# Splitting the scale-and-clamp of a row maximum: one VectorE operation added after the first half, one removed after the second

## The chip, the cores and the metric

The kernel runs on one core of one Trainium2 chip. The metric is device time in microseconds (us), the median of three runs. A core has five engines that run side by side, each with a queue that it works through in order: TensorE (PE, matrix products), VectorE (DVE), ScalarE (ACT), GpSimd (POOL) and SyncE (SP, which here issues every DMA). They wait for one another on semaphores.

## What is computed

A cross-attention block and a quantised feed-forward block, each behind a layer norm and with a residual, on x of 8 x 1024 x 512. Only the second block bears on the change:

```python
def _act_quant(x):
    scale = 127.0 / jnp.clip(jnp.max(jnp.abs(x), axis=-1, keepdims=True), 1e-05)
    xq = jnp.clip(jnp.round(x * scale), -128.0, 127.0) / scale
    return x + jax.lax.stop_gradient(xq - x)

def _bitlinear(x, w):
    return jnp.einsum('bsi,oi->bso', _act_quant(x), _weight_quant(w))
gate = jax.nn.silu(_bitlinear(x, w_gate))
up = _bitlinear(x, w_up)
return _bitlinear(gate * up, w_down)
```

`gate * up` is called h below. It is 2048 wide, and each of its rows is quantised by its own largest absolute value before the product with `w_down`.

## The kernel before

The 8192 rows are 64 tiles of 128 rows; a row lies in one SBUF partition. Weights stay on chip. A tile goes through two halves of the program, attention first and, six tiles behind, the feed-forward part, so that one turn of the loop works on several tiles at once. Of one tile the feed-forward part does this:

- `stats` and `rstd` (DVE, then POOL) find mean and inverse deviation; `x_scale` (DVE, L1085 to L1092) centres the row, finds its maximum and writes three scales, one of them `sgu[:, 1]`, by which `up` has to be multiplied; `quant_x` (ACT) and `copy_x` (DVE) quantise, and a DMA transposes.
- `gate_up` (PE, L1327) makes gate and up in four slices of 512 columns; `silu` (ACT, L818) and `mult` (DVE, L1032) turn each slice into a slice of h in SBUF, still without the scale of up.
- `h_part` (DVE, L1036) takes the absolute maximum of columns 0 to 1023 of h into `hm[:, 0:1]`, `h_max` (L1040) that of columns 1024 to 2047 into `hm[:, 1:2]`. L1041 joins both into `am`, L1042 multiplies by `sgu[:, 1]` and clamps from below at EPS into `t2`, L1044 inverts it and L1045 makes `c2`, the factor of the quantisation. All of these but the first work on one number in each partition.
- `quant_h` (ACT, L827) scales h by `c2`, `copy_h` (DVE, L1050) casts it, a DMA transposes it, `down` (PE, L1346) multiplies, and `final` (DVE, L1024) adds the result to the row. `d_scale` (POOL, L660) makes its scale from `t2`.

Of the attention half these pieces are met below: `e_sum` (DVE, L1073 to L1077), `p_norm` (POOL, L679), `p_hi` (ACT, L845), `p_lo` (POOL, L687), `add_bo` (POOL, L673), `add_x` (DVE, L1104), `x_norm` (DVE, L1056) and `s_max` (DVE, L1063 and L1067).

There is extra work in three blocks of eight tiles (the attention's weights are folded for two batches at once): `pair_X` on PE (L1254, L1259, which wait for `final`), `j_wide` (L781, L787) and `j_hi` (L794) on ACT, `j_lo` (L698) on POOL. The first block lies in the opening. Tiles with this work are called fold tiles here, the others plain tiles.

The order of each queue comes from `put(time, piece)`: pieces are sorted by a planned time. For the opening (up to about 340 us) the order is instead written out by hand, in a list for each engine. A piece is one function, and what it issues stays together. `link(...)` around a DVE operation counts a semaphore up at its end and makes the next DVE operation wait for it; without it, the next operation may begin before the last one has ended.

Of the kernel before, what the change touches and what calls it, by code (L numbers as in the profile page):

```python
# [13 lines left out]
EPS = 1e-5  # L14
L = 6
R = 11
W = 8

ALU = mybir.AluOpType
ACT = mybir.ActivationFunctionType  # L20
AX_X = mybir.AxisListType.X
# [7 lines left out]
def xattn_ffn(nc, x, ctx_768, Wq, Wk, Wv, Wo, bo, w_gate, w_up, w_down, out):  # L29
# [11 lines left out]
    with ExitStack() as ctx:  # L41
        def sb(name, shape, dt):
            return ctx.enter_context(nc.sbuf_tensor(name, shape, dt))
# [15 lines left out]
        h = FF[:, 0:4096].rearrange("p (s n) -> p s n", s=2)  # L59
# [61 lines left out]
        am = sb("am", [P, 2, W], F32)  # L121
        hm = sb("hm", [P, 4], F32)
# [3 lines left out]
        sgu = sb("sgu", [P, 2, W], F32)  # L126
        t2 = sb("t2", [P, W], F32)
# [768 lines left out]
        def _(eng):  # L896
# [3 lines left out]
            def link(ins):  # L900
                ch[0] += 1
                ins.then_inc(v_ch, 1)
                eng.wait_ge(v_ch, ch[0])
# [129 lines left out]

            def h_part(i):
                eng.wait_ge(v_h, 4 * i + 2)
                eng.tensor_reduce(hm[:, 0:1], h[:, i % 2, 0:1024], AX_X, ALU.max, apply_absolute_value=True)  # L1036

            def h_max(i):
                eng.wait_ge(v_h, 4 * i + 4)
                link(eng.tensor_reduce(hm[:, 1:2], h[:, i % 2, 1024:2048], AX_X, ALU.max, apply_absolute_value=True))  # L1040
                link(eng.tensor_tensor(am[:, 1, i % W:i % W + 1], hm[:, 0:1], hm[:, 1:2], ALU.max))  # L1041
                link(eng.tensor_scalar(t2[:, i % W:i % W + 1], am[:, 1, i % W:i % W + 1], sgu[:, 1, i % W:i % W + 1], EPS,  # L1042
                                       ALU.mult, ALU.max))
                link(eng.reciprocal(r2[:, i % W:i % W + 1], t2[:, i % W:i % W + 1]))  # L1044
                eng.tensor_scalar(c2[:, i % W:i % W + 1], r2[:, i % W:i % W + 1], sgu[:, 1, i % W:i % W + 1], 127.0, ALU.mult,  # L1045
                                  ALU.mult).then_inc(v_c2, 1)
# [88 lines left out]
            for s in range(FIRST, LAST + 1):  # L1135
                i, j = s, s + L
                if 0 <= i - 2 < NT:
                    put(at(s, .02) if s < NT - 1 else at(max(s, NT), (.122, .125, .127)[s - NT + 1]), final, i - 2)
                if 0 <= j + 1 < NT:
                    put(norm_at(s, .05, "stats"), stats, j + 1, 0)  # L1140
                if 0 <= i + 1 < NT:
                    put(x_at(i + 1, 0), stats, i + 1, 1)
                if 0 <= i - 1 < NT:
                    late = .41 if i == NT - 1 else 0
                    put(at(s, late + .11), copy_h, i - 1, 0)
                    put(at(s, late + .12), copy_h, i - 1, 1)
                if 0 <= j + 1 < NT:
                    put(norm_at(s, .3, "norm"), x_norm, j + 1)
                if 0 <= j < NT:
                    put(at(s, .4), s_max, j)  # L1150
                    put(at(s, .6), e_sum, j)
                if 0 <= i + 1 < NT:
                    put(x_at(i + 1, 2), x_scale, i + 1)
                    put(x_at(i + 1, 4), copy_x, i + 1)
                if 0 <= j - 1 < NT:
                    put(at(s, .8), add_x, j - 1)
                if 0 <= i < NT:
                    for f, w in enumerate((.15, .45, .65, .94)):
                        put(at(s, w), mult, i, f)
                    put(at(s, .62), h_part, i)  # L1160
                    put(at(s, .95), h_max, i)
# [233 lines left out]
```

## Time and profile before

| what | value |
|---|---|
| median of three runs | 1132.76 us (1132.17 to 1136.36) |
| profiled execution, its time | 1135.72 us |
| profiled execution, span of the core | 1133.9 us |
| PE, DVE, ACT, POOL busy | 94%, 88%, 66%, 44% |
| granted PE clock, mean of the profiled execution | 0.984 |
| maximum of h's first half (L1036) | 64 times, 1209 ns |
| maximum of h's second half (L1040) | 64 times, 1218 ns |
| joining both maxima (L1041) | 64 times, 527 ns |
| scale and clamp (L1042) | 64 times, 214 ns |

A row of a timeline has start, duration, engine, line, operation, what is written and read, and in brackets the idle time before it with what ended it. Consecutive DVE operations overlap a little where no wait stands between them, so the distance from one start to the next, and not the duration, is what an operation takes of its engine. A chain row names what the end of the run was waiting for at that moment.

### The profile page before, as it was taken

Reading aid. Unit: us, or ns where it says so; the run is one execution under the profiler, and the core shown is the slowest. Engines: PE = TensorE matmul, PEld = TensorE weight load, DVE = VectorE, ACT = ScalarE, POOL = GpSimd, SP = SyncE. Lnnn points to the kernel's source line nnn. Section 1 sums busy time; section 2 is a strip of 40 time slices with the busy share of each in tenths; the row PEclk is TensorE's granted clock in tenths of the full one; section 3 lists DMA queues with packets and bytes.
Section 4 is the critical chain, followed back from the end, with each engine's and each line's share of the span. In section 5 each row is a group of like instructions: output and inputs, shape, how many; then the busy total and the mean of one; then the engine's idle time right before and its main releaser. Section 6 shows DMA issues by size and latency. Waiting matters only on the chain.

```text
span 1133.9 us, 17119 instructions
## 1 busy us (share of the span) xinstructions
PE 1071.5 (94%) x5308; PEld 482.7 (43%) x5370; DVE 1003.0 (88%) x2097; ACT 744.4 (66%) x955; POOL 497.5 (44%) x641
## 2 busy tenths in 40 slices
PE   6668999999999999999999999999999999999998
PEld 3323344444344444444444444444444444444443
DVE  5888989978989998988999989889999999998886
ACT  2888657767756676676666666766766666665543
POOL 1046544556544445455443454454444444444110
PEclk9769999999999999999999999999999999999999
DMA  9798653564355454354455544544555544554334
GB/s 349 218 257 163 110 116 75 89 136 103 73 118 122 103 117 112 79 112 107 99 106 118 117 106 94 104 108 85 115 117 120 101 106 103 121 108 93 72 73 98
DMA packets 355962, 133.79 MB, mean 118 GB/s; under 512 B 332448, under 2 KB 332960, under 8 KB 355360
## 3 DMA queue, kind: packets, MB, share of 16 engines
q1 hardware_dynamic: 355872, 132.70, 53.1%
q8 instruction: 43, 0.70, 0.3%
q14 instruction: 47, 0.39, 0.1%
HBM read 34.08 MB, written 16.78 MB: 45 GB/s over the span
## 4 chain that ended last, share of the span: by engine, by line
PE 38%; DVE 19%; issue 6%; POOL 4%; ACT 4%; DMA 1%; SPq 0%; ACTq 0%; DVEq 0%; POOLq 0%
PE ps L1327 17%; PE ps L1346 8%; PE ps L1266 4%; PE ps L1267 4%; PE ps L1269 4%; DVE hm L1040 3%; DVE FF L1032 2%; DVE FF L1085 2%; POOL rs L653 2%; DVE bns L1018 1%; POOL MV L698 1%; DVE hm L1036 1%; ACT FF L818 1%; DVE xr L1024 1%; DVE am L1041 1%
## 5 line engine op out<-in xcount | busy, mean ns | idle before, releaser
L1327 PE MATMUL ps<-wgT,FF 128*128 128x512 bf16 x1024 | 262.9, 379 | 1.6 <-ACT FF L818 1.0
L1327 PE MATMUL ps<-wW,FF 128*128 128x512 bf16 x1024 | 262.9, 379 | 1.6 <-DVE FF L1032 1.6
L1346 PE MATMUL ps<-wW,FF 128*128 128x512 bf16 x962 | 218.7, 379 | 9.5 <-DMA FF<-FF 4.8
L827 ACT ACTIVATE FF<-FF,c 128x1024 int16<-128x1024 f32 x128 | 141.1, 1141 | 124.1 <-DVE c L1045 121.5
L818 ACT ACTIVATE FF<-ps,sgu 128x512 f32<-128x512 f32 x256 | 173.4, 680 | 63.5 <-PE ps L1327 62.0
L1032 DVE TENSOR_TENSOR FF<-FF,ps 128x512 f32<-128x512 f32 x256 | 173.4, 681 | 38.0 <-ACT FF L818 18.9
L679 POOL TENSOR_TENSOR AT<-AT,rd 128x512 f32<-128x512 f32 x64 | 67.4, 1053 | 298.3 <-DVE rd L1077 295.1
L1346 PEld LDWEIGHTS ps<-wW,FF 128*128 128x128 bf16 x1024 | 99.7, 98 | 128.4 <-issue 7.2
L1327 PEld LDWEIGHTS ps<-wW,FF 128*128 128x128 bf16 x1024 | 99.7, 98 | 123.9 <-DVE FF L1032 4.9
L1327 PEld LDWEIGHTS ps<-wgT,FF 128*128 128x128 bf16 x1024 | 98.8, 98 | 124.9 <-issue 3.2
L667 POOL TENSOR_TENSOR xhl<-xn,xhl 128x512 f16<-128x512 f32 x64 | 74.1, 1158 | 75.4 <-ACT xhl L834 75.4
L687 POOL TENSOR_TENSOR AT<-AT 128x512 f16<-128x512 f32 x64 | 74.6, 1166 | 50.3 <-POOL AT L679 37.3
L651 POOL TENSOR_SCALAR ve<-mv 128x1 f32<-128x1 f32 x128 | 45.2, 353 | 116.9 <-DVE mv L1019 116.9
L1018 DVE BATCH_NORM_STATS2 bns<-xr 128x6 f32<-128x512 f32 x128 | 86.3, 675 | 3.2 <-DMA xr<-in_x 3.1
L845 ACT ACTIVATE AT<-AT 128x512 f16<-128x512 f32 x64 | 40.1, 627 | 73.7 <-POOL AT L679 73.5
L653 POOL TENSOR_TENSOR rs<-ve,half 128x1 f32<-128x1 f32 x128 | 83.5, 652 | 10.7
L1266 PE MATMUL ps<-MV,xT 128*128 128x512 f16 x192 | 75.8, 395 | 10.3 <-DMA xT<-xhl 9.1
L673 POOL TENSOR_TENSOR xr<-xr,bo_sb 128x512 f32<-128x512 f32 x64 | 81.7, 1277 | 0.0
L1040 DVE TENSOR_REDUCE hm<-FF 128x1 f32<-128x1024 f32 x64 | 77.9, 1218 | 1.9
L1266 PE MATMUL ps<-MV,pT 128*128 128x512 f16 x192 | 73.6, 383 | 4.3 <-issue 2.9
L1036 DVE TENSOR_REDUCE hm<-FF 128x1 f32<-128x1024 f32 x64 | 77.4, 1209 | 0.1
L1267 PE MATMUL ps<-MV,xT 128*128 128x512 f16 x192 | 75.8, 395 | 0.0
(142 smaller groups left out, 1730.7 us busy)
## 6 DMA issues: line engine op xcount, KB each, us to landing
xr<-in_x SPq DMA_DIRECT2D x64, 256.0 KB, 2.8
out<-xr SPq DMA_DIRECT2D x64, 256.0 KB, 2.3
FF<-in_L_ffn_w_gate SPq DMA_DIRECT2D x4, 1024.0 KB, 13.4
wW<-in_L_ffn_w_up SPq DMA_DIRECT2D x4, 1024.0 KB, 14.2
FF<-in_L_ffn_w_down SPq DMA_DIRECT2D x4, 1024.0 KB, 6.1
FF<-FF SPq DMA_TRANSPOSE x192, 3.2
MV<-in_L_xattn_Wq SPq DMA_DIRECT2D x1, 1024.0 KB, 5.7
MV<-in_L_xattn_Wo SPq DMA_DIRECT2D x1, 1024.0 KB, 12.3
```

The costliest lines, as they stand in the source:

```text
L653: eng.tensor_tensor(rs[:, t % W:t % W + 1], ve[:, t % W:t % W + 1], half[:, :], ALU.pow).then_inc(end, 1)
L673: eng.tensor_tensor(xr[:, t % R, :], xr[:, t % R, :], bo_sb[:, :], ALU.add).then_inc(g_xb, 1)
L818: eng.activation(h[:, i % 2, f * 512:(f + 1) * 512], G[n % 2][:, :], ACT.Silu, scale=sgu[:, 0, i % W:i % W + 1]).then_inc(a_si, 1)
L827: eng.activation(q16h[:, 1024 * z:1024 * z + 1024], h[:, t % 2, 1024 * z:1024 * z + 1024], ACT.Copy, scale=c2[:, t % W:t % W + 1]).then_in ...
L1018: link(eng.bn_stats(bns[:, k, t % 2, :], xr[:, t % R, :]))
L1032: eng.tensor_tensor(hh, hh, U[n % 2][:, :], ALU.mult).then_inc(v_h, 1)
L1036: eng.tensor_reduce(hm[:, 0:1], h[:, i % 2, 0:1024], AX_X, ALU.max, apply_absolute_value=True)
L1040: link(eng.tensor_reduce(hm[:, 1:2], h[:, i % 2, 1024:2048], AX_X, ALU.max, apply_absolute_value=True))
L1266: eng.matmul(bank[:, :], T[:, k, :], hi[k], start=(k == 0), stop=False)
L1267: eng.matmul(bank[:, :], T[:, k, :], lo[k], start=False, stop=False)
L1327: mm = eng.matmul(bank[n % 2][:, :].rearrange("p (o f) -> p o f", o=4), qxT[:, i % 2, k, :], w[:, 4 * f:4 * f + 4, k, :], start=(k == 0), ...
L1346: mm = eng.matmul(y_bank(i)[:, :], hT[:, i % 2, c, :], wdT[:, c, :], start=(c == 0), stop=(c == 15))
```

## The change

`h_part` now waits for its own maximum, by a link, and then multiplies it by `sgu[:, 1]` and clamps it at EPS, into `hm[:, 2:3]`. In `h_max` the operation that joined the two maxima is gone; the following one multiplies the second maximum by `sgu[:, 1]` and takes the larger of that and `hm[:, 2:3]`. It has two scalars read from SBUF, where it had one and a constant. `am` is no longer written there. PE, ACT, POOL and SP have the same instructions in the same order.

```diff
             def h_part(i):
                 eng.wait_ge(v_h, 4 * i + 2)
-                eng.tensor_reduce(hm[:, 0:1], h[:, i % 2, 0:1024], AX_X, ALU.max, apply_absolute_value=True)
+                link(eng.tensor_reduce(hm[:, 0:1], h[:, i % 2, 0:1024], AX_X, ALU.max, apply_absolute_value=True))
+                eng.tensor_scalar(hm[:, 2:3], hm[:, 0:1], sgu[:, 1, i % W:i % W + 1], EPS, ALU.mult, ALU.max)
 
             def h_max(i):
                 eng.wait_ge(v_h, 4 * i + 4)
                 link(eng.tensor_reduce(hm[:, 1:2], h[:, i % 2, 1024:2048], AX_X, ALU.max, apply_absolute_value=True))
-                link(eng.tensor_tensor(am[:, 1, i % W:i % W + 1], hm[:, 0:1], hm[:, 1:2], ALU.max))
-                link(eng.tensor_scalar(t2[:, i % W:i % W + 1], am[:, 1, i % W:i % W + 1], sgu[:, 1, i % W:i % W + 1], EPS,
+                link(eng.tensor_scalar(t2[:, i % W:i % W + 1], hm[:, 1:2], sgu[:, 1, i % W:i % W + 1], hm[:, 2:3],
                                        ALU.mult, ALU.max))
```

The DVE queue around `h_part` of a fold tile, before:

```order
L1092 TENSOR_SCALAR c<-r,rs 128x1
L1036 TENSOR_REDUCE hm<-FF 128x1
L1032 TENSOR_TENSOR FF<-FF,ps 128x512
L1099 CAST FF<-FF 128x512
L1073 TENSOR_REDUCE den<-AT 128x8
```

And after:

```order
L1092 TENSOR_SCALAR c<-r,rs 128x1
L1036 TENSOR_REDUCE hm<-FF 128x1
L1037 TENSOR_SCALAR hm<-hm,sgu 128x1
L1032 TENSOR_TENSOR FF<-FF,ps 128x512
L1099 CAST FF<-FF 128x512
L1073 TENSOR_REDUCE den<-AT 128x8
```

The scale and clamp of the first half now stands between its maximum and the third `mult`. The DVE queue around `h_max` of the same tile, before:

```order
L1104 SCALAR_TENSOR_TENSOR xr<-ps,bck,xr 128x512
L1032 TENSOR_TENSOR FF<-FF,ps 128x512
L1040 TENSOR_REDUCE hm<-FF 128x1
L1041 TENSOR_TENSOR am<-hm 128x1
L1042 TENSOR_SCALAR t<-am,sgu 128x1
L1044 RECIPROCAL r<-t 128x1
L1045 TENSOR_SCALAR c<-r,sgu 128x1
L1024 SCALAR_TENSOR_TENSOR xr<-ps,sd,xr 128x512
```

And after (the second maximum is now on line 1041 of the file):

```order
L1104 SCALAR_TENSOR_TENSOR xr<-ps,bck,xr 128x512
L1032 TENSOR_TENSOR FF<-FF,ps 128x512
L1041 TENSOR_REDUCE hm<-FF 128x1
L1042 TENSOR_SCALAR t<-hm,sgu 128x1
L1044 RECIPROCAL r<-t 128x1
L1045 TENSOR_SCALAR c<-r,sgu 128x1
L1024 SCALAR_TENSOR_TENSOR xr<-ps,sd,xr 128x512
```

One operation fewer stands between the second maximum and `c2`; the rest of the queue is as it was.

## Rows read from the trace of the kernel before

**Rows 1.** The page: busy time of each engine, share of the span, instructions.

```profile
PE 1071.5 (94%) x5308; PEld 482.7 (43%) x5370; DVE 1003.0 (88%) x2097; ACT 744.4 (66%) x955; POOL 497.5 (44%) x641
```

**Rows 2.** Stretches of one tile: length, busy PE, PEld, DVE, ACT, POOL; clock, DMA.

```profile
624.05:639.59 15.54, 15.49 (x73) 7.05 (x72) 14.46 (x31) 9.98 (x12) 6.75 (x10) 1.00 0.59 111
...
705.30:722.61 17.31, 16.44 (x97) 7.66 (x96) 15.25 (x31) 12.36 (x18) 9.02 (x12) 1.00 0.54 100
...
773.99:791.02 17.03, 16.43 (x85) 7.27 (x85) 15.25 (x31) 12.15 (x16) 9.01 (x12) 1.00 0.50 102
```

**Rows 3.** Chain that ended last, in a fold tile: start us, length us, what.

```profile
717.14 1.04 DVE hm L1036
...
722.61 0.65 DVE am L1041
...
731.51 1.41 DVE FF L1085
```

**Rows 4.** Timeline of DVE in the same fold tile.

```profile
717.06 1.21 DVE L1036 TENSOR_REDUCE hm<-FF 128x1 f32<-128x1024 f32 x1
718.18 0.68 DVE L1032 TENSOR_TENSOR FF<-FF,ps 128x512 f32<-128x512 f32 x1
...
722.61 0.64 DVE L1041 TENSOR_TENSOR am<-hm 128x1 f32<-128x1 f32 x1
723.29 0.21 DVE L1042 TENSOR_SCALAR t<-am,sgu 128x1 f32<-128x1 f32 x1
723.53 0.16 DVE L1044 RECIPROCAL r<-t 128x1 f32<-128x1 f32 x1
723.73 0.21 DVE L1045 TENSOR_SCALAR c<-r,sgu 128x1 f32<-128x1 f32 x1
723.86 0.74 DVE L1024 SCALAR_TENSOR_TENSOR xr<-ps,sd,xr 128x512 f32<-128x512 f32 x1
```

**Rows 5.** Timeline of POOL in the same fold tile.

```profile
722.08 1.15 POOL L687 TENSOR_TENSOR AT<-AT 128x512 f16<-128x512 f32 x1 [0.80 <-POOL AT L679]
723.20 1.26 POOL L673 TENSOR_TENSOR xr<-xr,bo_sb 128x512 f32<-128x512 f32 x1
...
725.50 0.21 POOL L651 TENSOR_SCALAR ve<-mv 128x1 f32<-128x1 f32 x1 [0.76 <-DVE mv L1019]
...
731.47 1.16 POOL L698 TENSOR_TENSOR MV<-FF,MV 128x512 f16<-128x512 f32 x1 [0.99 <-ACT MV L794]
```

**Rows 6.** A DVE group with constants only: busy us, mean ns; idle before it.

```profile
L1003 DVE TENSOR_SCALAR wst<-wst 128x1 f32<-128x1 f32 x3 | 0.5, 153 | 0.1
```

**Rows 7.** PE's waits from 400 to 1080 us: total us, times, longest.

```profile
PE ps L1259 <- DVE xr L1024: 5.0, 8, 0.8
```

**Rows 8.** Timeline of DVE in the opening, small operations beside a POOL operation.

```profile
286.71 0.21 DVE L1088 TENSOR_SCALAR t<-am,rs 128x1 f32<-128x1 f32 x1
...
287.15 0.68 DVE L1091 TENSOR_SCALAR sgu<-wst,t 128x2 f32<-128x2 f32 x1
```

**Rows 9.** Timeline of POOL at the same time.

```profile
286.65 1.16 POOL L687 TENSOR_TENSOR AT<-AT 128x512 f16<-128x512 f32 x1
```

**Rows 10.** L1041 and L1085: shortest, median and longest of 64 in ns.

```profile
L1041 DVE TENSOR_TENSOR am<-hm x64: 158/641/1087, 124.6 to 1121.0; 128x1 f32<-128x1 f32 x64
...
L1085 DVE TENSOR_SCALAR FF<-xr,mv x64: 448/481/1530, 94.5 to 1104.3; 128x512 f32<-128x512 f32 x64
```

**Rows 11.** Timeline of DVE in the opening: a long L1041.

```profile
155.50 1.09 DVE L1041 TENSOR_TENSOR am<-hm 128x1 f32<-128x1 f32 x1
```

**Rows 12.** Chain between opening and first full block of fold tiles.

```profile
361.49 1.20 DVE hm L1036
...
365.23 0.17 DVE am L1041
```

**Rows 13.** Chain over the last tiles.

```profile
1068.15 0.17 DVE am L1041
...
1118.52 0.52 issue
```

## What I predict

> **What bounds the kernel now.** I read the engines' shares first. PE is busy for 94% of the span and DVE for 88% [rows 1], which leaves open who waits for whom, so the next view is one tile at a time. There are two sorts of tile. A plain tile takes 15.54 us, and PE is busy in 15.49 of them [rows 2]: there PE sets the pace, and the chain that ended last, followed through such a stretch, consists of PE lines alone. A saving on DVE is worth nothing there. A fold tile takes 17.31 us (17.03 in the later ones of a block, where `pair_X` has its second form), and PE is busy for 16.44 of it [rows 2]. PE stands still in it, 0.8 us at a time, in front of `pair_X`, waiting for `final` on DVE [rows 7]. In a fold tile the chain goes round in a loop: down DVE from `x_scale` (L1085) over `h_part` (L1036), `e_sum`, `add_x`, `mult` and `h_max` to L1041 and L1042, then over `final`, `stats` and `rstd`, a `j_lo`, the next `j_wide` and `silu`, and back to L1085 [rows 3]. So in the fold tiles, and not in the others, what DVE does between the two maxima and `c2` is time.
>
> The second thing to see is what L1041 costs. It takes the larger of two numbers in each partition, and it lasts from 158 to 1087 ns, median 641 [rows 10]. In the fold tile it begins at 722.61 and ends at 723.25 [rows 4]. POOL's `p_lo` began at 722.08 and lasted 1.15 us, to 723.23 [rows 5]. In the fold tiles, L1041 ends 0.02 us after `p_lo`: it is held by it, and the hold is three quarters of its time. The Trainium skill (SBUF — State Buffer, section Who interferes with whom) gives a mechanism: a DVE instruction with two SBUF inputs contends with a GpSimd instruction that reads SBUF, and the later one blocks until the first is done. L1041 reads two SBUF tensors, so the trace agrees, with 0.64 us held against 0.16 free.
>
> **The change part by part.**
>
> *The joined maximum goes.* From the start of L1041 to that of L1042 it takes 723.29 - 722.61 = 0.68 us in a fold tile [rows 4]; where nothing holds it, 0.16 + 0.04 = 0.20 us.
>
> *L1042 reads a second scalar from SBUF.* No tiny operation with two of them is in the trace. The bounds: nothing, if both are fetched together; and what the first one costs, 214 ns of L1042 [rows 4] less 153 ns of L1003 with constants only = 61 ns [rows 6]. I take 0.06 us, the same step again. So L1041's removal is worth 0.68 - 0.06 = 0.62 us where it was held and 0.14 us where it wasn't.
>
> *Is the new form held in its turn?* Without L1041 the scale and clamp stands inside `p_lo`'s time. In the opening L1088, of the same shape (128x1, one scalar from SBUF), began at 286.71 inside a `p_lo` that ran from 286.65 to 287.81, and took its usual 0.21 us; L1091 (128x2) began at 287.15 in the same `p_lo` and took 0.68 us, to its end [rows 8, 9]. And L1042, L1044 and L1045 now lie inside `add_bo`, which begins at 723.20, with nothing lost [rows 4, 5]. So one-element operations with one tensor are not held.
>
> *`h_part` grows by an operation and a wait.* Now the next operation starts 718.18 - 717.06 = 1.12 us after it, before it has ended [rows 4]. With the link it must end: 1.21 us, then the 0.03 us that lie between L1042's end and L1044's start, then the new operation, which takes 723.86 - 723.73 = 0.13 us from its start to the next one's, as L1045 does [rows 4]. Together 1.37 us, 0.25 more. Behind it on DVE stand the third `mult`, `copy_x`, `e_sum`, `add_x`, the last `mult` and `h_max`; for these wait ACT, PE and, on `e_sum`, POOL's `p_norm` and `p_lo`.
>
> *A fold tile:* -0.62 + 0.25 = -0.37 us. There are two blocks of eight on the chain, 410 to 531 us and 670 to 792 us; L1041 lies on it 16 times, L1036 14 times (rows 3 show one of each): 16 x 0.62 - 14 x 0.25 = 9.9 - 3.5 = 6.4 us. What becomes late next? PE waits 0.8 us for `final`, so it has 0.8 to give. POOL is idle for 0.76 us before `rstd` (L651) [rows 5]; its `p_lo` and `add_bo` come 0.25 later and DVE's `stats` 0.37 earlier against the start of the loop, so 0.76 - 0.62 = 0.14 us is left. Thin, but enough.
>
> *Between the opening and the first block (340 to 410 us)* the chain has four more L1041, two free ones as at 365.23 and two held, and one L1036 whose full 1.20 us count already [rows 12]: 2 x 0.14 + 2 x 0.61 - (1.37 - 1.20) = 1.3 us.
>
> *The last tiles* have four free L1041 on the chain, 4 x 0.14 = 0.6 us; the last `h_part` has 0.52 us of idle behind it, which covers its 0.25 [rows 13].
>
> *Plain tiles:* nothing. PE is the pace, and DVE, at 14.46 of 15.54 us [rows 2], gains 0.37 of slack. Were that cover gone, the price would be 0.
>
> *The opening (120 to 340 us, 13 tiles)* has its order written out by hand, and the chain can't be followed through it. Four L1041 are held there (0.59 to 1.09 us, [rows 11] is the longest), nine are free. If every L1041 counted and no `h_part`, it would give about 3.7 - 0.24 + 9 x 0.14 = 4.7 us; if every `h_part` counted and no L1041, it would cost 13 x 0.25 = 3.3 us. A hold removed here may also pass to the next cast or `x_norm`. I take 0, near the middle, and keep both ends.
>
> **The sum:** 6.4 + 1.3 + 0.6 + 0 = 8.3 us. From the profiled execution's 1135.72 us that gives 1127.4. That execution lies 3.0 us above the median of the runs, 1132.76, and the median is what I forecast: 1132.76 - 8.3 = 1124.5 us.
>
> **The rivals.**
>
> *The opening pays.* The fold tiles give their 6.4 us, the tiles around them 1.9, and the opening takes all of its 3.3: 1132.8 - 5.0 = 1127.7 us, which is within 0.5%. For it: DVE is as busy there as elsewhere. Against it: four holds of up to 1.09 us go in the same stretch.
>
> *The hold passes to the scale and clamp.* L1042 would start 0.68 earlier and 0.25 later, at 722.86 in the clock of rows 4, and end with `p_lo`, itself 0.25 later, at 723.48; now it ends at 723.50. The fold tiles would gain nothing, and I would get 1132 us. Rows 8 and 9 speak against it, since L1088 is the same form. The Trainium skill (VectorE: DVE Perf Modes, section What auto-detection actually checks) bears on this: a one-source operation in SBUF takes both ports if the outermost non-unit dimensions are even or equal. Read so that one element counts as equal, it would make L1042 contend; the 128x2 row agrees with the rule and the 128x1 row with the reading that one element doesn't qualify.
>
> *POOL becomes the loop (slower).* The place is POOL between `p_norm` and `rstd` in the fold tiles. Its operations hang on `e_sum`, which comes 0.25 us later. The slack there is 0.14 us by my count, and POOL's durations are rough; if it is used up, by more than 0.14 us of extra POOL time, the gain after L1041 ends in POOL's queue. At full size the loop then runs from `h_part` over `p_norm` to `rstd` and carries the 0.25 with no gain: 16 x 0.25 = 4.0 us, and with the opening's 3.3 it is 1132.8 + 7.3 = 1140.1 us. Against it: POOL is busy for only 9.02 of 17.31 us [rows 2].
>
> *A second hold falls too (much faster).* `x_scale`'s L1085 begins at 731.51 [rows 3] and lasts 1.41 us because POOL's L698 began at 731.47 [rows 5], 0.04 us ahead. Its median over the run is 0.48 [rows 10]. If DVE came first, a fold tile would save another 0.9 us: 14 x 0.9 = 13 us, 1111.9. Against it: both hang on the same `silu`, so both move together.
>
> **How the numbers follow.** Forecast 0.61, the opening pays 0.19, the hold passes on 0.05, POOL becomes the loop 0.09, the second hold falls 0.06. The opening's own bounds put the forecast between 1132.8 - 13.0 = 1119.8 and 1127.8. A range from 1119 to 1133 holds the forecast and the first two rivals, 0.85, and leaves out the slower case and the much faster one. A measurement can tell about 0.5%, or 5.7 us, from no change. The faster side is the forecast, less a little of its upper end, and the last rival, 0.64; the same side is the first two rivals and that upper end, 0.27; slower 0.09.
>
> **What would show it.** Right: no `am<-hm` operation; fold tiles of about 16.94 and 16.66 us and plain tiles still at 15.54; the distance from the second maximum's start to `c2` about 0.6 us shorter; t2's operation at 0.21 to 0.28 us; L1036 to the next operation 1.37; PE's wait before `pair_X` near 0.45 and POOL's idle before L651 near 0.14. Wrong: t2's operation at 0.6 us (the hold has passed on); POOL with no idle time before L651, and fold tiles at 17.3 or more; or an opening that has become over 3 us longer. If plain tiles change at all, my reading that PE alone bounds them is wrong.

## The result

| | median | lowest to highest | runs |
|---|---|---|---|
| before | 1132.76 us | 1131.46 to 1136.36 | 5 |
| changed kernel | 1123.41 us | 1121.14 to 1126.73 | 5 |

The ratio is 0.9913, with a 95% interval of 0.9884 to 0.9941: the kernel became faster by 0.6 to 1.2%. Forecast were 1124.5 us. A second comparison on another occasion gave 1122.22 against 1131.25 us, ratio 0.993 (0.9906 to 0.9954).

The shares of the changed kernel, which answer to [rows 1] (busy time, share of the span, instructions). DVE has the same number of instructions as before and 16 us less to do:

```profile
PE 1066.2 (95%) x5308; PEld 481.0 (43%) x5370; DVE 987.3 (88%) x2097; ACT 745.1 (66%) x955; POOL 498.5 (44%) x641
```

Stretches of one tile in it, as in [rows 2]: two fold tiles, of the first and second form, and a plain tile.

```profile
695.20:712.16 16.96, 16.91 (x99) 7.87 (x98) 14.89 (x31) 12.37 (x18) 9.04 (x12) 1.00 0.55 102
745.80:762.47 16.67, 16.43 (x85) 7.29 (x84) 14.89 (x32) 12.15 (x16) 9.03 (x12) 1.00 0.47 103
614.60:630.14 15.54, 15.49 (x73) 7.02 (x73) 14.06 (x32) 9.98 (x12) 6.76 (x10) 1.00 0.55 111
```

The fold tiles went from 17.31 to 16.95 us and from 17.03 to 16.67; the plain tile kept its 15.54 although DVE does 0.4 us less in it. The DVE timeline of a fold tile, to be laid beside [rows 4]:

```profile
706.36 1.21 DVE L1036 TENSOR_REDUCE hm<-FF 128x1 f32<-128x1024 f32 x1
707.60 0.21 DVE L1037 TENSOR_SCALAR hm<-hm,sgu 128x1 f32<-128x1 f32 x1
707.73 0.68 DVE L1032 TENSOR_TENSOR FF<-FF,ps 128x512 f32<-128x512 f32 x1
...
710.19 0.68 DVE L1032 TENSOR_TENSOR FF<-FF,ps 128x512 f32<-128x512 f32 x1
710.90 1.22 DVE L1041 TENSOR_REDUCE hm<-FF 128x1 f32<-128x1024 f32 x1
712.16 0.27 DVE L1042 TENSOR_SCALAR t<-hm,sgu 128x1 f32<-128x1 f32 x1
712.47 0.16 DVE L1044 RECIPROCAL r<-t 128x1 f32<-128x1 f32 x1
```

From L1036 to the third `mult` it is now 707.73 - 706.36 = 1.37 us, as forecast. From the start of the scale and clamp to L1044 it is 712.47 - 712.16 = 0.31 us, where L1041 and L1042 together had taken 723.53 - 722.61 = 0.92 in [rows 4]. That operation begins inside `p_lo`, which runs from 711.63 to 712.79, and isn't held:

```profile
711.63 1.16 POOL L687 TENSOR_TENSOR AT<-AT 128x512 f16<-128x512 f32 x1 [0.80 <-POOL AT L679]
712.75 1.28 POOL L673 TENSOR_TENSOR xr<-xr,bo_sb 128x512 f32<-128x512 f32 x1
714.00 0.31 POOL L660 TENSOR_SCALAR sd<-t,wst 128x1 f32<-128x1 f32 x1
714.44 0.21 POOL L651 TENSOR_SCALAR ve<-mv 128x1 f32<-128x1 f32 x1
...
715.92 0.57 POOL L653 TENSOR_TENSOR rs<-ve,half 128x1 f32<-128x1 f32 x1
717.14 1.15 POOL L698 TENSOR_TENSOR MV<-FF,MV 128x512 f16<-128x512 f32 x1 [0.65 <-ACT MV L794]
```

Of the 64 executions of this scale and clamp 49 begin while an operation of POOL is running. All 64 (shortest, median, longest in ns) are alike:

```profile
L1042 DVE TENSOR_SCALAR t<-hm,sgu x64: 272/273/275, 118.9 to 1107.8; 128x1 f32<-128x1 f32 x64
```

PE waits for `final` in front of `pair_X` for 0.4 to 0.5 us at most, where it was 0.8 in [rows 7]; 0.45 was forecast.

To see where the time went I followed one event, the start of `c2`'s operation, through all 64 tiles of each trace and compared the distances with those of before (the column "before" has its time in us, the others the difference to it; minus is less time):

| stretch | before | changed | changed, second profile | share in the forecast |
|---|---|---|---|---|
| start to tile 0 | 125.2 | -5.8 | -6.4 | none |
| tiles 0 to 13 (opening) | 224.9 | -0.8 | -1.3 | 0 |
| 13 to 17 | 61.2 | -0.8 | -0.8 | -1.3 |
| 17 to 29 (block of fold tiles) | 198.3 | -2.9 | -2.9 | -3.2 |
| 29 to 33 (plain) | 62.2 | 0.0 | 0.0 | 0 |
| 33 to 45 (block of fold tiles) | 198.3 | -2.9 | -2.9 | -3.2 |
| 45 to 57 (plain) | 186.5 | +0.1 | +0.1 | 0 |
| 57 to 63 (end) | 65.1 | -0.4 | -0.5 | -0.6 |
| 0 to 63 together | 996.5 | -7.6 | -8.3 | -8.3 |

The first row isn't the change's, but for some tenths: the only changed operations in it are tile 0's own `h_part` and `h_max`, and from the start of its second maximum to `c2` it is 1.75 us instead of 1.88. Tile 0's `x_scale`, ahead of which nothing of the change runs, already began at 89.4 and 88.5 us instead of 94.5. What that is, is looked at in the experiments.

### The profile page after: what moved, and what is told of

It is laid out like the page before. It is cut to its first block, busy times and chain, and to the rows that moved or that the text cites. A ratio compares the mean times of both kernels' runs of the same rounds, so it can differ in the third digit from the quotient of the medians.

```text
span 1120.6 us, 17119 instructions
## 1 busy us (share of the span) xinstructions
PE 1066.2 (95%) x5308; PEld 481.0 (43%) x5370; DVE 987.3 (88%) x2097; ACT 745.1 (66%) x955; POOL 498.5 (44%) x641
## 4 chain that ended last, share of the span: by engine, by line
PE 49%; DVE 15%; POOL 3%; issue 3%; ACT 2%; DMA 1%; ACTq 0%; SPq 0%; DVEq 0%; POOLq 0%
PE ps L1327 22%; PE ps L1346 11%; PE ps L1266 5%; PE ps L1269 5%; PE ps L1267 5%; DVE FF L1032 2%; DVE hm L1041 2%; DVE FF L1085 2%; DVE hm L1036 2%; POOL rs L653 1%; POOL MV L698 1%; DVE xr L1024 1%; DVE am L1086 1%; DVE xr L1104 1%; DVE bns L1018 1%
## 5 line engine op out<-in xcount | busy, mean ns | idle before, releaser
L679 POOL TENSOR_TENSOR AT<-AT,rd 128x512 f32<-128x512 f32 x64 | 67.4, 1053 | 306.8 <-DVE rd L1077 303.7
L667 POOL TENSOR_TENSOR xhl<-xn,xhl 128x512 f16<-128x512 f32 x64 | 74.1, 1158 | 74.2 <-ACT xhl L834 74.2
L687 POOL TENSOR_TENSOR AT<-AT 128x512 f16<-128x512 f32 x64 | 74.6, 1166 | 49.5 <-POOL AT L679 37.3
L651 POOL TENSOR_SCALAR ve<-mv 128x1 f32<-128x1 f32 x128 | 45.5, 356 | 99.1 <-DVE mv L1019 96.8
L653 POOL TENSOR_TENSOR rs<-ve,half 128x1 f32<-128x1 f32 x128 | 83.7, 654 | 10.7
L1266 PE MATMUL ps<-MV,xT 128*128 128x512 f16 x192 | 75.8, 395 | 7.5 <-DMA xT<-xhl 6.4
L673 POOL TENSOR_TENSOR xr<-xr,bo_sb 128x512 f32<-128x512 f32 x64 | 81.9, 1281 | 0.0
L1041 DVE TENSOR_REDUCE hm<-FF 128x1 f32<-128x1024 f32 x64 | 78.0, 1218 | 1.9
L1036 DVE TENSOR_REDUCE hm<-FF 128x1 f32<-128x1024 f32 x64 | 77.4, 1209 | 0.1
L834 ACT ACTIVATE xhl<-xn 128x512 f16<-128x512 f32 x64 | 40.0, 626 | 54.5 <-DVE xn L1056 49.6
## 6 DMA issues: line engine op xcount, KB each, us to landing
FF<-in_L_ffn_w_gate SPq DMA_DIRECT2D x4, 1024.0 KB, 13.3
```

The source lines that it names most:

```text
L653: eng.tensor_tensor(rs[:, t % W:t % W + 1], ve[:, t % W:t % W + 1], half[:, :], ALU.pow).then_inc(end, 1)
L673: eng.tensor_tensor(xr[:, t % R, :], xr[:, t % R, :], bo_sb[:, :], ALU.add).then_inc(g_xb, 1)
L687: eng.tensor_tensor(phl[:, 1, :], E[:, j % 2, :], phl[:, 0, :], ALU.subtract).then_inc(g_pl, 1)
L1036: link(eng.tensor_reduce(hm[:, 0:1], h[:, i % 2, 0:1024], AX_X, ALU.max, apply_absolute_value=True))
L1266: eng.matmul(bank[:, :], T[:, k, :], hi[k], start=(k == 0), stop=False)
```

## The experiments

The theory to test has three parts: L1041 was slow because GpSimd held it; `h_part`'s new wait costs 0.25 us on the path of a fold tile; POOL is close to becoming the bound there. Rivals are that it is one operation and one wait fewer that counted, that the new wait is hidden, and that the hold had another cause.

### Only the join, without a second SBUF tensor

```diff
-link(eng.tensor_tensor(am[:, 1, i % W:i % W + 1], hm[:, 0:1], hm[:, 1:2], ALU.max))
+link(eng.tensor_scalar(am[:, 1, i % W:i % W + 1], hm[:, 1:2], hm[:, 0:1], None, ALU.max))
```

> The kernel before with one edit: L1041 joins the two maxima as an operation with one SBUF tensor and one scalar read from SBUF, in place of one with two SBUF tensors. Number of operations, waits and h_part are as before. My theory (L1041 is slow because a GpSimd operation that reads SBUF holds it): L1041 falls from a median of 641 ns to about 214 ns and is never held; start of L1041 to start of L1042 goes from 0.68 to 0.25 us, fold tiles from 17.31 to 16.88 and from 17.03 to 16.60 us, plain tiles stay at 15.54; in all about 16 x 0.43 = 6.9 us plus under 1 us around the blocks: 1125 us, ratio 0.993. Rival (what counted was one operation and one semaphore wait fewer ahead of c2): L1041 stays near 0.64 us, fold tiles 17.31 and the ratio 1.000.

Measured: 1123.7 us against 1130.61, ratio 0.9934 (0.9915 to 0.9953). Fold tiles 16.90 and 16.62 us. L1041 in all its runs, against [rows 10]:

```profile
L1041 DVE TENSOR_SCALAR am<-hm x64: 213/214/215, 119.4 to 1107.3; 128x1 f32<-128x1 f32 x64
```

With the number of operations and waits unchanged, the same join is 0.43 us shorter (median 214 ns for 641) and the fold tiles by 0.41. That settles it against the rival: what counted was the kind of operand, not the number of operations. The whole effect of the change can be had from this one line: from tile 0 to tile 63 it gives 8.5 us, where the change gives 7.6 and 8.3.

### Only the first half of the change

```diff
 def h_part(i):
-    eng.tensor_reduce(hm[:, 0:1], h[:, i % 2, 0:1024], AX_X, ALU.max, apply_absolute_value=True)
+    link(eng.tensor_reduce(hm[:, 0:1], h[:, i % 2, 0:1024], AX_X, ALU.max, apply_absolute_value=True))
+    eng.tensor_scalar(hm[:, 2:3], hm[:, 0:1], sgu[:, 1, i % W:i % W + 1], EPS, ALU.mult, ALU.max)
```

> The kernel before with the first half of the change alone: h_part waits for its maximum and makes the scaled and clamped value, which nobody reads; h_max is as before, with the held L1041. My sum: L1036 to the operation behind it but one 1.37 us instead of 1.12, fold tiles 17.56 and 17.28 us, 14 x 0.25 = 3.5 us more in the blocks, and between 0 and 3.3 us more in the opening: 1136 to 1139 us, ratio 1.003 to 1.006. Rival (the wait is hidden, because DVE idles later in the tile waiting for silu): fold tiles stay at 17.31, ratio 1.000.

Measured: 1137.04 us against 1130.61, ratio 1.0049 (1.0031 to 1.0067). Fold tiles 17.57 and 17.29 us, each 0.26 longer; the two blocks +1.9 us each. PE waits longer for `final` (total us, times, longest), against the 5.0 and 0.8 of [rows 7]:

```profile
PE ps L1260 <- DVE xr L1024: 7.0, 8, 1.1
```

So the price of the added wait and operation is as worked out, and it is paid on the path. But between tiles 0 and 13 the distance changed by 0.04 us in all, and between 13 and 17 by 0.05. Single tiles of the opening moved by up to 0.6 us either way, and two profiles of one kernel differ there by 0.5 to 0.8 us; so the wait costs well under the 3.3 us of the bound, and whether it costs exactly nothing can't be told.

### POOL has less to do, and DVE waits longer

```diff
-eng.tensor_tensor(phl[:, 1, :], E[:, j % 2, :], phl[:, 0, :], ALU.subtract).then_inc(g_pl, 1)
+n = 512 if j == 0 else 128
+eng.tensor_tensor(phl[:, 1, 0:n], E[:, j % 2, 0:n], phl[:, 0, 0:n], ALU.subtract).then_inc(g_pl, 1)
```

> The kernel before, with p_lo on POOL (L687) working on 128 of its 512 columns from the second tile on; the rest of the low half keeps what the first tile left there, so a part of the attention's low-order product is left out. DVE's instructions are the same. In a fold tile p_lo is followed at once by add_bo, which takes 1.26 us and also reads SBUF. If L1041 is held by whichever GpSimd operation is reading when it starts: p_lo ends before L1041 starts, add_bo begins some 0.7 us earlier and holds it in its place, until about 723.7 in the clock of the tile shown: L1041 gets LONGER, to 1.0 to 1.1 us instead of 0.64, and the fold tiles go to about 17.7 us, though POOL has less to do. Rival (L1041 waits for p_lo alone, by some dependence on it): 0.16 us and fold tiles of 16.8. Rival (its length has nothing to do with POOL): 0.64 us and 17.31.

Measured: 1142.92 us against 1131.57, ratio 1.0098 (1.0074 to 1.0122); fold tiles 17.82 and 17.55 us. POOL in a fold tile:

```profile
707.74 0.43 POOL L688 TENSOR_TENSOR AT<-AT 128x128 f16<-128x128 f32 x1 [0.80 <-POOL AT L679]
708.12 1.27 POOL L673 TENSOR_TENSOR xr<-xr,bo_sb 128x512 f32<-128x512 f32 x1
```

and the join (here L1042) beside it on DVE, with its durations over all runs:

```profile
708.26 1.14 DVE L1042 TENSOR_TENSOR am<-hm 128x1 f32<-128x1 f32 x1
...
L1042 DVE TENSOR_TENSOR am<-hm x64: 159/1139/1146, 120.9 to 1126.7; 128x1 f32<-128x1 f32 x64
```

`p_lo` takes 0.43 us instead of 1.15 and ends before the join starts; `add_bo` has begun 0.14 us ahead of it, runs to 709.39, and the join ends at 709.40. The hold doesn't belong to `p_lo` but to the GpSimd operation that is running when the join starts. The trace of before has it too: 47 of its 64 L1041 end 0.01 to 0.02 us behind the end of a POOL operation, on five different lines (L667, L673, L679, L687, L698), and the 15 that begin outside any take 158 to 160 ns. All five read and write SBUF, so no run here separates reading from writing. Taking work from POOL made the kernel 1% slower. The hold on two SBUF inputs is the behaviour that the Trainium skill states (SBUF — State Buffer, Who interferes with whom) for a DVE instruction with two SBUF inputs against a GpSimd instruction that reads SBUF; the trace agrees, with the join's end 0.01 us behind that of `add_bo`.

### The scale and clamp without its wait

The changed kernel, with the new operation moved from `h_part` to the head of `h_max` (not shown: `part_done = [0]` ahead of it, and the rest of `h_max`, which is unchanged):

```diff
 def h_part(i):
-    link(eng.tensor_reduce(hm[:, 0:1], h[:, i % 2, 0:1024], AX_X, ALU.max, apply_absolute_value=True))
-    eng.tensor_scalar(hm[:, 2:3], hm[:, 0:1], sgu[:, 1, i % W:i % W + 1], EPS, ALU.mult, ALU.max)
+    eng.tensor_reduce(hm[:, 0:1], h[:, i % 2, 0:1024], AX_X, ALU.max, apply_absolute_value=True).then_inc(v_ch, 1)
+    ch[0] += 1
+    part_done[0] = ch[0]
 def h_max(i):
+    eng.wait_ge(v_ch, part_done[0])
+    eng.tensor_scalar(hm[:, 2:3], hm[:, 0:1], sgu[:, 1, i % W:i % W + 1], EPS, ALU.mult, ALU.max)
```

> The changed kernel, but the scale and clamp of the first half's maximum isn't made in h_part: it stands at the head of h_max, just ahead of the second maximum, where the first maximum is long there. h_part has no wait any more. If my 0.25 us for h_part is right and is paid on the path: the new operation fits in the 0.1 us in which DVE waits for the last mult anyway, so fold tiles go from 16.95 to about 16.70 to 16.75 and from 16.67 to 16.42 to 16.5, in all 3 to 4 us below the changed kernel: about 1120 us, ratio to before 0.989. PE then waits about 0.2 us for final in a fold tile, so it is near its floor. Rival (POOL, whose idle time before L651 is down to 0.13 us in the changed kernel, has become the bound): fold tiles stay at 16.9, ratio 0.991.

Measured: 1117.13 us against 1130.61, ratio 0.9872 (0.985 to 0.9894). Fold tiles 16.70 and 16.43 us. DVE around the place:

```profile
706.92 0.68 DVE L1033 TENSOR_TENSOR FF<-FF,ps 128x512 f32<-128x512 f32 x1
707.52 0.21 DVE L1043 TENSOR_SCALAR hm<-hm,sgu 128x1 f32<-128x1 f32 x1
707.64 1.21 DVE L1045 TENSOR_REDUCE hm<-FF 128x1 f32<-128x1024 f32 x1
```

From the last `mult` to the maximum it is 707.64 - 706.92 = 0.72 us; in the changed kernel it is 710.90 - 710.19 = 0.71 without the operation. The operation is free here: DVE would otherwise stand until the `mult` has ended. The fold tiles came as expected, so the rival, POOL as the bound at 16.9, falls. These are two stretches of one fold tile each:

```profile
692.40:709.10 16.70, 16.70 (x99) 7.76 (x98) 14.71 (x32) 12.37 (x18) 9.03 (x12) 1.00 0.56 104
742.50:758.93 16.43, 16.43 (x86) 7.23 (x84) 14.72 (x32) 12.15 (x16) 9.04 (x12) 1.00 0.48 105
```

PE is busy for the whole of them, the chain that ended last runs through PE lines alone, and of the 0.2 us that PE was still to wait for `final` the view of its waits shows nothing. But 16.70 us isn't PE's own time. The chain has `pair_X` of the same tile and of the next (start us, length us, what):

```profile
694.21 0.78 PE ps L1258 x24
...
710.63 0.78 PE ps L1258 x24
```

That is 16.42 us from one to the next. The 16.70 is the distance from one `c2` to the next, so DVE's loop takes 0.28 us more than PE's work does. `c2` enters the second block 2.26 us ahead of `pair_X`. That lead shrinks to 1.73 us over a first distance of 16.95, and to 1.45, 1.16 and 1.02 us over the next three of 16.70. It just lasts until the tiles of the second form, where both take 16.43. So PE's pace is the bound of the block, to within 0.2 us for the seven distances between its eight `pair_X`, though `c2`'s distance doesn't show it.

### The clamp behind the reciprocal

The kernel before; `h_part` untouched, `sgu` with a third column for the scale over 127. Not shown are the lines that make this column, and `d_scale`, which now reads a weight scale that isn't divided by 127 and takes `t2` without the clamp; that differs only for a row whose scaled maximum lies under EPS:

```diff
-link(eng.tensor_tensor(am[:, 1, i % W:i % W + 1], hm[:, 0:1], hm[:, 1:2], ALU.max))
-link(eng.tensor_scalar(t2[:, i % W:i % W + 1], am[:, 1, i % W:i % W + 1], sgu[:, 1, i % W:i % W + 1], EPS,
-                       ALU.mult, ALU.max))
+link(eng.tensor_scalar(t2[:, i % W:i % W + 1], hm[:, 1:2], hm[:, 0:1], sgu[:, 2, i % W:i % W + 1],
+                       ALU.max, ALU.mult))
 link(eng.reciprocal(r2[:, i % W:i % W + 1], t2[:, i % W:i % W + 1]))
-eng.tensor_scalar(c2[:, i % W:i % W + 1], r2[:, i % W:i % W + 1], sgu[:, 1, i % W:i % W + 1], 127.0, ALU.mult,
-                  ALU.mult).then_inc(v_c2, 1)
+eng.tensor_scalar(c2[:, i % W:i % W + 1], r2[:, i % W:i % W + 1], 127.0 / EPS, sgu[:, 1, i % W:i % W + 1],
+                  ALU.min, ALU.mult).then_inc(v_c2, 1)
```

> The kernel before with the clamp moved: h_part as before; h_max takes the larger of both maxima and multiplies by the scale over 127 in one operation with two scalars read from SBUF; the clamp is made behind the reciprocal, in the operation that makes c2. So L1041 goes and nothing is added in the loop. Expected by my sum: 0.62 us per fold tile, 16.69 and 16.41 us, 16 x 0.62 = 9.9 us less in the blocks and some in the opening; PE waits 0.2 us in a fold tile. About 1121 us, ratio 0.989, 3 to 4 us below the changed kernel. Rival (POOL or PE bounds the fold tile by now): 16.9 us, ratio 0.991.

Measured: 1120.16 us against 1130.61, ratio 0.9906 (0.9886 to 0.9926); fold tiles 16.71 and 16.43 us, as in the kernel before this one. The rival at 16.9 falls here too. One operation fewer than that one in each tile buys nothing more: there the extra operation was free on DVE, and PE is the pace of the block in both. In total it is 3.0 us behind it, with intervals that overlap. Of the 5.4 us between the two profiled executions 3.8 lie ahead of tile 0's `c2`, 0.5 in the second block, where PE waits once for 0.64 us for a DMA, and 1.1 in the last tiles.

### The changed kernel again

No edit.

> The changed kernel once more, beside the two kernels below, on one chip. Ratio to before 0.991 to 0.993 as in the first comparison. Its fold tiles, 16.95 and 16.67 us, come out alike to 0.02 us; the time of the first tile's c2, which nothing of the change precedes, lies anywhere from 119 to 125 us as in the other executions so far, if that part is the setup's own scatter, and at 119.4 again if the change moves it.

> The changed kernel with the first half's scale and clamp at the head of h_max, once more, for a comparison with the changed kernel on one chip. If the h_part wait costs 0.25 us per fold tile and the opening about 1 us: 4 to 6 us below the changed kernel, ratio to before 0.987. If the first comparison had luck in the setup: the same tile times, but a ratio near 0.989.

Measured, on one chip: changed kernel 1122.22 us, ratio 0.993 (0.9906 to 0.9954); scale and clamp moved 1119.31 us, ratio 0.9899 (0.9878 to 0.9919); before 1131.25 us. The fold tiles are the same to 0.01 us as in the first profiles. The move is worth 2.9 us here, less than the 4 to 6 expected. From tile 0 to 63 the traces have 3.3: 3.4 in the two blocks, and nothing (0.2 more time) in the opening, where I had looked for 1. The first two profiles had 4.6, with 3.3 in the blocks and 1.1 in the opening, so the opening's part isn't settled by these; the blocks' part is. The expectation also says that nothing of the change precedes tile 0's `c2`; as said above, tile 0's own `h_part` and `h_max` do.

On the start: tile 0's `x_scale` and `c2` began at these times in the ten profiles, beside PE's granted clock and number of matmuls from 60 to 90 us:

| kernel | `x_scale` | `c2` | clock | matmuls |
|---|---|---|---|---|
| moved, second profile | 86.8 | 117.3 | 0.83 | 152 |
| changed, second profile | 88.5 | 118.8 | 0.83 | 144 |
| changed | 89.4 | 119.4 | 0.78 | 140 |
| moved | 89.6 | 119.5 | 0.83 | 140 |
| only the join | 89.6 | 120.1 | 0.83 | 140 |
| less POOL work | 90.8 | 121.5 | 0.77 | 113 |
| clamp behind the reciprocal | 93.0 | 123.3 | 0.72 | 84 |
| changed, with more POOL work (below) | 93.7 | 124.2 | 0.73 | 86 |
| only the first half | 93.6 | 124.2 | 0.73 | 86 |
| before | 94.5 | 125.2 | 0.73 | 84 |

The windows of before and of the changed kernel (columns as in [rows 2]):

```profile
60.00:90.00 30.00, 17.07 (x84) 6.14 (x82) 24.62 (x53) 24.67 (x29) 14.83 (x18) 0.73 1.08 247
...
60.00:90.00 30.00, 19.03 (x140) 7.61 (x141) 24.80 (x56) 24.52 (x30) 18.22 (x22) 0.78 1.03 246
```

Three of the profiles have the changed kernel's instructions up to `c2`: 118.8, 119.4 and 124.2 us. So the setup scatters by some 5 us from one execution to the next. Of the 13.3 us between the two profiled spans, 1133.9 and 1120.6, 5.8 lie ahead of tile 0's `c2`, and 5.2 of them are there already at its `x_scale`: that is scatter, not gain. Why the setup is quick in one execution and slow in another wasn't tried.

### POOL at its supposed decision point

```diff
 eng.tensor_scalar(sd[:, i % W:i % W + 1], t2[:, i % W:i % W + 1], wst[:, 2, 3:4], None,
                   ALU.mult).then_inc(g_sd, 1)
+eng.tensor_scalar(am[:, 1, i % W:i % W + 1], t2[:, i % W:i % W + 1], wst[:, 2, 3:4], None, ALU.mult)
```

> The changed kernel with a second, unused d_scale-like operation on POOL right behind d_scale (L660): same shape, some 0.3 us of POOL time, ahead of rstd (L651). It tests the slower rival, POOL as the bound of a fold tile, at its decision point. In the changed kernel POOL is idle for 0.13 us there. If that is the slack, 0.17 us of the added 0.3 comes through to the loop: fold tiles 17.12 and 16.84 us, 14 x 0.17 = 2.4 us more in the blocks, ratio to before about 0.994. If POOL has more slack than the trace shows: 16.95 and the ratio of the changed kernel. If it had none: 17.25.

Measured: 1125.2 us, ratio 0.9934 (0.9911 to 0.9958), and fold tiles of 16.95 and 16.67 us: no effect in the blocks at all. POOL in such a tile:

```profile
717.34 0.31 POOL L660 TENSOR_SCALAR sd<-t,wst 128x1 f32<-128x1 f32 x1
717.62 0.29 POOL L662 TENSOR_SCALAR am<-t,wst 128x1 f32<-128x1 f32 x1
717.87 0.22 POOL L651 TENSOR_SCALAR ve<-mv 128x1 f32<-128x1 f32 x1
718.17 0.66 POOL L653 TENSOR_TENSOR rs<-ve,half 128x1 f32<-128x1 f32 x1
...
720.48 1.16 POOL L699 TENSOR_TENSOR MV<-FF,MV 128x512 f16<-128x512 f32 x1 [0.61 <-ACT MV L795]
```

From `d_scale` to `j_lo` it is 720.48 - 717.34 = 3.14 us, and 3.14 in the changed kernel without the operation as well (714.00 to 717.14). The idle time that stands before `j_lo`, 0.65 us in the changed kernel, is 0.61 now; `j_lo` waits for ACT's `j_hi`. The expectation fell. But the test was milder than meant. From `d_scale` to L651 it is 0.53 us instead of 0.44, so only 0.09 us of the delay was left there, and the second L653 ended 2.52 us behind `d_scale` instead of 2.49, since the operations between had become shorter (0.76 to 0.66 and 0.55 to 0.49 us). The run shows that so much doesn't reach the tile; how much would isn't measured.

## Why the prediction was right, point by point

**What bounds the kernel.** Right in the main. Plain tiles stayed at 15.54 us with DVE's path up to 0.6 us shorter and 0.25 us longer; only with 0.5 us more of hold did they become 15.58. For the fold tiles the part of the loop on DVE, from `x_scale` to `c2`, was right; the part behind `c2` wasn't, as said under POOL below.

**The hold.** Right, and now shown from two sides: another kind of operand removes it (214 ns), another GpSimd operation takes it over (1139 ns).

**The second scalar.** Taken at 0.06 us; L1042 went from 214 to 273 ns, 0.059.

**The new form isn't held.** Right in 64 of 64 executions, 49 of them begun beside a running POOL operation, so the rival by which the hold passes on is out. By the Trainium skill's rule (VectorE: DVE Perf Modes, What auto-detection actually checks) a one-source operation in SBUF takes both ports if the outermost non-unit dimensions are even or equal. The rows fit the reading that one element a partition doesn't qualify: none of those was held, while L1091, with two elements, takes 227 to 231 ns in 59 of 64 executions and up to 1198 ns in the other five, all of which begin beside a POOL operation. Which port an operation took is in no trace.

**`h_part`.** Taken at 0.25 us more; 1.37 us measured, and 0.26 per fold tile where it was added alone.

**A fold tile.** -0.37 forecast, -0.36 measured (16.95 and 16.67 for 16.94 and 16.66). The blocks gave 2.9 us each and not 3.2, because the first tile of a block gave 0.19 instead of the 0.62 that I counted for a tile with only L1041 on the chain; the way out of a block gave another 0.2. In the changed kernel the first three `pair_X` of the second block start at 663.82, 680.24 and 696.73 us, 16.42 and 16.49 apart: there PE's own pace holds, and only then does the loop with its 16.95.

**340 to 410 us.** Mis-sized: 0.8 us for 1.3. I had added up L1041s on the chain as if each could be shortened in full without another wait taking over. Tiles 15 and 16 did give 0.62 and 0.73 us, but tile 17 went from 15.06 to 15.54, PE's pace in a plain tile, and took 0.48 back.

**The opening.** I took 0 and kept -4.7 to +3.3. It was -0.8 and -1.3 in two profiles of the same kernel, and -2.1 in the one with more POOL work, which has the same DVE instructions. The upper bound was far too high: 13 waits of 0.25 us cost 0.04 us together when they were added alone, and one and the same DVE queue scatters there by 1.4 us. The rival in which the opening pays 3.3 us is refuted by both; its time, 1132.8 - 5.0, should read 1127.8.

**The last tiles.** 0.6 forecast, 0.4 and 0.5 measured.

**POOL as the next bound.** The step that failed, though the sum didn't hang on it. I read POOL's idle time ahead of L651 as its slack, 0.14 us after the change, and 0.13 is there. But 0.28 us more work went in without a trace of it in the tile time. The chain that I followed led through `rstd` to `j_lo`, with an "issue" piece of 0.62 us between them. The timelines of the kernel before show another path from the same `c2`, which ends at 723.94 [rows 4], to the same `j_lo`. On ACT, `quant_h`, `silu`, `j_wide` and `j_hi`:

```profile
723.98 2.19 ACT L827 ACTIVATE FF<-FF,c 128x1024 int16<-128x1024 f32 x2 [2.03 <-DVE c L1045]
726.08 0.67 ACT L818 ACTIVATE FF<-ps,sgu 128x512 f32<-128x512 f32 x1
726.64 0.82 ACT L787 ACTIVATE FF<-ps,fwd 128x256 f32<-128x256 f32 x2
727.50 0.63 ACT L794 ACTIVATE MV<-FF 128x512 f16<-128x512 f32 x1
```

and on POOL the end of `rstd`, and `j_lo`:

```profile
726.98 0.57 POOL L653 TENSOR_TENSOR rs<-ve,half 128x1 f32<-128x1 f32 x1
728.21 1.16 POOL L698 TENSOR_TENSOR MV<-FF,MV 128x512 f16<-128x512 f32 x1 [0.65 <-ACT MV L794]
```

ACT works without a gap from `c2` to 728.13, and `j_lo`, whose only wait in the program is for `j_hi`, starts 0.08 us later; `rstd` has been over for 0.66 us. So the loop goes over ACT here, and `final`, `stats` and `rstd` lie beside it, with that much to spare on POOL. A chain that crosses half a microsecond of nothing has taken the wrong branch. The sum was right all the same, since both branches start from `c2` and what the change touches stands ahead of it. Nothing was run that lengthens or shortens ACT's part alone.

**The second hold.** `x_scale` still takes 1.39 to 1.40 us in a fold tile and starts 0.04 to 0.05 us behind POOL's operation. The order didn't flip.

**The total.** Tile by tile the gain is 7.6 to 8.3 us for 8.3 forecast. The medians differ by 9.4 and 9.0; the rest is within their intervals, and the setup alone scatters by more.

## What to carry to other kernels

A tiny operation whose duration varies as this one's did, from 158 to 1087 ns, is likely held by something: lay its end beside the ends of the other engines' operations before changing the algorithm around it. Here the cure was to pass one of two one-column operands as a scalar, and a value needed later costs nothing if it is made where the engine waits anyway (just ahead of an operation with a wait of its own), but the full 0.25 us if it is put where it needs a wait of its own (0.12 for the wait, 0.13 for the operation). Measure an engine's pace by its own events: `c2` came every 16.70 us while PE did a tile in 16.42. Once PE is busy for all of a block, stop: the last operation saved on DVE gave nothing.

## What the runs showed of the hardware

- A DVE operation with two tensors in SBUF, one element a partition each, that starts beside a 128x512 GpSimd operation lasts until that one's end (47 of 64, to 0.02 us; five different lines). So with 0.72 us of work taken from POOL the held operation grew from 641 to 1139 ns.
- The same maximum with one of the two passed as a scalar was never held: 213 to 215 ns in 64 of 64 executions.
- Reading a second scalar from SBUF costs a one-element DVE operation 59 ns, nearly what the first one costs (61 ns, [rows 4, 6]).
- The setup of one and the same instruction stream reached tile 0's `c2` at 118.8, 119.4 or 124.2 us. Over all ten profiles the four slowest had a mean granted PE clock of 0.72 to 0.73 from 60 to 90 us and the others 0.77 to 0.83.
